# Folding products moved into the lead-in, value products waited for by halves, and reciprocal roots placed between the last scatters

## The reference, cut to what matters

```python
# x: 32 x 56 x 128; ctx: 32 x 1500 x 128; 16 heads of 8
h = layernorm(x)
q, k, v = h @ Wq + bq, ctx @ Wk + bk, ctx @ Wv + bv
att = softmax(where(causal[56, 1500] & mask, q k^T / sqrt(8), -1e9))
x = x + (att v) @ Wo + bo
# mixture of experts, 8 experts, 2 per token, capacity 280
xf = layernorm(x)
probs = softmax(xf @ gate_w + gate_b); top 2, renormalised
rank = cumsum over tokens of (token chose expert); slots past capacity dropped
h = relu(xin @ w1[e] + b1[e]); out = (h @ w2[e] + b2[e]) * weight
x = x + scatter_add(out)
```

## Time and profile before

| | |
|---|---|
| time, median of 3 runs | 176.41 us (176.31 to 176.62) |
| profiled execution, own time | 177.93 us |
| its span | 176.2 us |
| mean granted TensorE clock in it | 0.934 of 2.4 GHz |
| busy: PE (matmul) / PEld (weight loads) | 148.6 / 101.8 us |
| busy: DVE / ACT / POOL | 113.2 / 85.7 / 88.3 us |

### The profile page before, as it was taken

One profiled execution on the slowest core, in us unless ns is written; L12 is line 12 of the kernel. 1 busy time (PEld: TensorE's weight loads), 2 busy tenths in 40 slices (PEclk: granted clock), 3 DMA queues, 4 the chain that ended last, 5 costly groups with the idle time before them and its releaser, 6 DMA issues.

```text
span 176.2 us, 4560 instructions
## 1 busy us (share of the span) xinstructions
PE 148.6 (84%) x1623; PEld 101.8 (58%) x1623; DVE 113.2 (64%) x421; ACT 85.7 (49%) x188; POOL 88.3 (50%) x145
## 2 busy tenths in 40 slices
PE   6979999999999989999899796949999999894000
PEld 2436486686666767566666652414778888683000
DVE  3587747868888888787979866004385665642361
ACT  3468787589696987969766310000433333320000
POOL 5304980513586776857567466750044444656000
PEclk9999999879999999999999969996999999999555
DMA  5990299499910000001000000007300110103476
GB/s 156 335 379 4 81 407 330 127 339 335 270 53 20 31 29 9 23 13 31 15 4 26 0 22 5 22 13 199 97 15 30 37 39 15 55 24 100 180 246 228
DMA packets 10542, 19.14 MB, mean 109 GB/s; under 512 B 2044, under 2 KB 6000, under 8 KB 9880
## 3 DMA queue, kind: packets, MB, share of 16 engines
q1 hardware_dynamic: 7424, 15.12, 25.5%
q0 software_dynamic: 1632, 2.28, 4.1%
q10 hardware_dynamic: 1464, 1.45, 2.7%
HBM read 12.13 MB, written 7.91 MB: 114 GB/s over the span
## 4 chain that ended last, share of the span: by engine, by line
PE 47%; ACT 14%; issue 13%; DVE 9%; POOL 7%; DMA 6%; POOLq 1%; DVEq 0%; SPq 0%; ACTq 0%
PE bank L1250 7%; PE score_p L1049 6%; PE bank L1077 5%; ACT probsT L570 4%; ACT head_keys L514 4%; POOL slots_d L419 4%; PE score_p L1232 4%; PE bank L1232 4%; PE bank L1064 3%; PE score_p L981 3%; PE score_p L1016 3%; DMA chosen<-choice_d 2%; DMA choice_d<-rest_ow,rest_i 2%; DVE row_max L688 2%; ACT probs L561 2%
## 5 line engine op out<-in xcount | busy, mean ns | idle before, releaser
L419 POOL DMA_INDIRECT slots_d<-rec,slot_i x32 | 32.3, 1009 | 14.4 <-issue 9.3
L465 POOL DMA_INDIRECT choice_d<-ow,dst_i x16 | 15.8, 987 | 25.2 <-DVE ow L939 22.2
L981 PE MATMUL score_p<-warm 128*128 128x512 bf16 x76 | 23.1, 461 | 4.5 <-DMA slots_d<-rec,slot_i 2.4
L688 DVE TENSOR_REDUCE row_max<-score_p 128x16 f32<-128x912 f32 x16 | 17.7, 1107 | 4.8 <-PE score_p L1049 4.7
L570 ACT ACTIVATE probsT<-bank 128x512 f32<-128x512 f32 x32 | 17.6, 605 | 5.2 <-PE bank L1064 4.9
L1049 PE MATMUL score_p<-head_keys,queries 32*32 32x228 f32 (+1 forms) x384 | 19.6, 366 | 0.4 <-ACT head_keys L514 0.4
L1077 PE MATMUL bank<-vals,probsT 128*64 128x18 f32 x512 | 17.6, 212 | 2.4 <-ACT probsT L570 2.4
L1077 PEld LDWEIGHTS bank<-vals,probsT 128*64 128x64 f32 x512 | 16.1, 138 | 6.0 <-ACT probsT L570 4.5
L691 DVE TENSOR_TENSOR probs<-score_p,row_max 128x912 f32<-128x912 f32 x16 | 17.7, 1109 | 1.6
L1064 PE MATMUL bank<-ident,probs 128*128 128x128 f32 x128 | 17.7, 283 | 0.0
L981 PEld LDWEIGHTS score_p<-warm 128*128 128x128 bf16 x76 | 8.3, 114 | 15.8 <-issue 5.8
(11 more groups left out here) (153 smaller groups left out, 267.1 us busy)
## 6 DMA issues: line engine op xcount, KB each, us to landing
choice_d<-chosen SPq DMA_DIRECT2D x2, 1024.0 KB, 8.3
w_s<-w_in SPq DMA_DIRECT2D x1, 2048.0 KB, 9.6
slots_d<-keys_c SPq DMA_DIRECT2D x1, 1260.0 KB, 4.5
xg<-slots_d SPq DMA_DIRECT2D x8, 140.0 KB, 3.2
xT<-x_t_in SPq DMA_DIRECT2D x1, 1024.0 KB, 10.6
chosen<-choice_d SPq DMA_DIRECT2D x1, 1024.0 KB, 5.4
xs<-x_in SPq DMA_DIRECT2D x1, 768.0 KB, 7.4
ctxT<-ctx_t_in SPq DMA_DIRECT2D x1, 768.0 KB, 8.7
```

What stands on the lines that cost most here:

```text
L419: gp.indirect_dma_start(out=slots_d, out_offset=bass.IndirectOffsetOnAxis(ap=slot_i[:, t, k, p:p + 1], axis=0), in_=rec[:, GP * t + p, :], ...
L688: ve.reduce_max(row_max[:, p, :], heads, X).then_inc(max_d, 1)
L981: mm(to, warm[:, 0:128], warm[:], start=True, stop=True)
```

## The change

- `fold_gate` and `share_logits` move from round 1 (behind values(0)) in front of the loop, where the 5 fillers stood. `centre_gate` moves from behind scores(1) in front of it, and one filler there goes. The transposed mean gets a bank of the ring for norm(2) instead of one of the post banks, with a semaphore of its own; norm(2) now waits until it has been copied. VectorE's copies follow: gate_c in front of softmax(1), fold and shareT in front of softmax(2), statistics1(3) behind softmax(2).
- `mix(n)` waits for the first half of the probabilities in front of product 1 and for the second in front of product 17.
- In round 7, ranks(5) goes in front of output(6) and slots(5) in front of residual(6); the post banks' order follows, so that mix(14) must wait until slots(5) has read its ranks.
- GpSimd's end: power2(6) between the first and the second DMA of scatter(5), power2(7) between the second and third of scatter(6). count(6) goes to VectorE (`count_late`), behind slots(6) and before weigh_late(6).
- Fillers: other numbers, and three new places (in front of rank 6, behind output(7) with a wait for root 7, and behind the arrival of the first expert's rows).

```diff
-WARM_LEAD = (3, 2, 2, 3)
-WARM_START, WARM_PAIR = 11, 5
-WARM_TURN, WARM_MIX, WARM_Y, WARM_CHOICE, WARM_SLOTS, WARM_SCATTER, WARM_LANDING, WARM_FIRST = 2, 2, 2, 14, 3, 27, 11, 4
+WARM_START, WARM_LEAD = 11, (3, 2, 2, 2)
+WARM_TURN, WARM_TAKEN, WARM_MIX, WARM_Y, WARM_LOGITS, WARM_CHOICE, WARM_SLOTS = 2, 3, 2, 3, 12, 7, 3
+WARM_SCATTER, WARM_LANDING, WARM_ROWS, WARM_FIRST = 32, 9, 3, 4
...
# GpSimd
-                if g >= 1:
+                if 1 <= g < GROUPS - 1:
                     power2(g - 1)
             t = GROUPS - 1
             count(t - 2)
-            scatter(t - 2)
+            scatter(t - 2, 0, 1)
+            power2(t - 1)
+            scatter(t - 2, 1)
+            scatter(t - 1, 0, 2)
             power2(t)
-            count(t - 1)
-            scatter(t - 1)
+            scatter(t - 1, 2)
             scatter(t)
...
# VectorE
+            def count_late(t):
+
+                dve.wait_ge(post_d, posted("rank", t))
+                for p in range(GP):
+                    dve.wait_ge(earlier_d, GP * t + p + 1)
+                    ve.tensor_tensor(earlier[:], earlier[:], taken[:, p, :], add).then_inc(earlier_d, 1)
...
                 softmax(GP * g + 1)
+                if g == GROUPS - 1:
+                    slots(g - 2)
                 residual(g - 1)
...
             slots(t - 1)
+            count_late(t - 1)
             weigh_late(t - 1, 0)
...
# TensorE
             def mix(n):
-                pe.wait_ge(probT_ev, 2 * n + 2)
                 pe.wait_ge(ring_ev, filled("v", t))
                 to = take_post("mix", n)
                 for hp in range(HP):
+                    if hp % 4 == 0:
+                        pe.wait_ge(probT_ev, 2 * n + 1 + hp // 4)
...
             project(1)
+            centre_gate()
             keep_warm(WARM_LEAD[3], probT_b[1][:])
             scores(1)
             pe.wait_ge(mean_done, 1)
-            tr(post("mean", 0)[:, 0:B], mean[:], ident[0:B, 0:B]).then_inc(post_d, 1)
-            centre_gate()
+            pe.wait_ge(ring_ev, filled("norm", 1))
+            tr(ring("norm", 2)[:, 0:B], mean[:], ident[0:B, 0:B]).then_inc(mean_d, 1)
             transpose_probs(0)
             transpose_probs(1)
-            keep_warm(WARM_PAIR, ring("norm", 1)[:])
+            fold_gate()
+            share_logits()
...
                     values(0)
-                    fold_gate()
-                    share_logits()
...
+                if g == GROUPS - 1:
+                    ranks(g - 2)
                 output(g - 1)
                 mix(GP * g)
-                if g >= 2:
+                if 2 <= g < GROUPS - 1:
                     ranks(g - 2)
...
             mix(PAIRS - 1)
+            keep_warm(WARM_TAKEN)
             ranks(t - 1)
             keep_warm(WARM_MIX)
             turn_y(t)
             keep_warm(WARM_Y)
             output(t)
+            keep_warm(WARM_LOGITS)
+            pe.wait_ge(rs2_d, GROUPS)
             keep_warm(WARM_CHOICE)
             ranks(t)
...
             keep_warm(WARM_LANDING)
+            pe.wait_ge(xg_in[0], 16)
+            keep_warm(WARM_ROWS)
             transpose_slots(0, 0)
```

More of the change, by code:

```diff
@@ L65, in post_order @@
 def post_order():
-    uses = [("kept", 0), ("mean", 0), ("centre", 0), ("fold", 0), ("shareT", 0), ("share", 0), ("mix", 0)]
+    uses = [("kept", 0), ("centre", 0), ("fold", 0), ("shareT", 0), ("share", 0), ("mix", 0)]
     for g in range(1, GROUPS):
-        for kind, t in (("mix", 2 * g - 1), ("wo", g - 1), ("mix", 2 * g), ("rank", g - 2)):
+        behind = (("wo", g - 1), ("mix", 2 * g))
+        rank = (("rank", g - 2),)
+        for kind, t in (("mix", 2 * g - 1), *(rank + behind if g == GROUPS - 1 else behind + rank)):
             if t >= 0:
@@ L201, in build @@
         wqk_in, mask_in, wvo_in, wb_in, consts_in = (sem(n) for n in ("wqk_in", "mask_in", "wvo_in", "wb_in", "consts_in"))
-        mean_done, meanT_ev, slow_dma, slow_step = (sem(n) for n in ("mean_done", "meanT_ev", "slow_dma", "slow_step"))
+        mean_done, mean_d, meanT_ev = (sem(n) for n in ("mean_done", "mean_d", "meanT_ev"))
+        slow_dma, slow_step = sem("slow_dma"), sem("slow_step")
         slots_cleared, choices_cleared, zeros_done, empties_done = (
@@ L786, in slots, with mean_column @@
                     ve.reduce_sum(slot_i[:, t], slot_k[:], X).then_inc(slot_d, 1)
[L788 to L793, removed]
+            def count_late(t):
[3 more added lines that the diff above has]
+                    ve.tensor_tensor(earlier[:], earlier[:], taken[:, p, :], add).then_inc(earlier_d, 1)
+            def mean_column(batches):
+                dve.wait_ge(mean_d, 1)
+                ve.tensor_copy(ctxT[:, batches, S], ring("norm", 2)[:, batches]).then_inc(meanT_ev, 1)
             ve.memset(warm[:], 1.0).then_inc(warm_done, 1)
@@ L831, in _ @@
             statistics1(2)
+            dve.wait_ge(post_d, posted("centre", 0))
+            dve.wait_ge(gate_clear, 1)
+            ve.tensor_copy(gate_c[:, 0:E], post("centre", 0)[:, 0:E]).then_inc(post_read, 1)
             softmax(1)
@@ L835, in _ @@
             dve.wait_ge(ctx_in[1], 16)
-            mean_column(slice(0, 4 * GP), False)
-            statistics1(3)
+            mean_column(slice(0, 4 * GP))
             dve.wait_ge(ctx_in[2], 16)
[L839 to L842, removed]
+            mean_column(slice(4 * GP, B))
+            dve.wait_ge(post_d, posted("fold", 0))
+            ve.tensor_copy(bo_share[:], post("fold", 0)[:, E:E + 1]).then_inc(bo_share_d, 1)
+            ve.tensor_copy(wvo_s[:, WVO_FOLD:WVO_FOLD + E], post("fold", 0)[:, 0:E]).then_inc(post_read, 1)
+            dve.wait_ge(bo_share_d, 1)
+            dve.wait_ge(post_d, posted("shareT", 0))
+            ve.tensor_scalar(shareT[:], post("shareT", 0)[:], bo_share[:], None, add).then_inc(post_read, 1)
             for g in range(1, GROUPS):
@@ L845, in _ @@
                 if g == 1:
[L846 to L849, removed]
-                    dve.wait_ge(post_d, posted("shareT", 0))
-                    ve.tensor_scalar(shareT[:], post("shareT", 0)[:], bo_share[:], None, add).then_inc(post_read, 1)
+                    statistics1(3)
                     dve.wait_ge(post_d, posted("share", 0))
@@ L984, in norm @@
                 pe.wait_ge(xn_d, GP * (t + 1))
+                if t == 2:
+                    pe.wait_ge(meanT_ev, 2)
                 transposes(take_ring("norm", t), xn).then_inc(ring_d, 1)
```

## The result

The changed kernel takes 174.04 us (median of 4 executions, 173.87 to 174.77). The kernel before took 176.51 us in the same set (176.31 to 180.66). The ratio is 0.989, with a 95% interval of 0.9845 to 0.9938: 1.1% faster. Medians here take in every execution; the ratios leave out those more than 1.5% above the fastest of their kernel. Forecast were 175.1 us, range 174.0 to 176.8. The profiled execution took 174.77 us (span 173.1, mean granted clock 0.969); the forecast for such an execution, without a low stretch in the round from 33.00, was 175.1.

A forecast was written before the change was run, and what follows sets the result against it. TensorE was taken to bound the loop, busy 10.31 of 10.75 us per round. From the profiled 177.93, - 1.2 - 0.96 + 0.95 - 0.96 gave 175.76; less 0.64 for the low stretch, 175.1 us, range 174.0 to 176.8.

The forecast's parts named there:

- the two front terms: Lead-in and value products: Term A and Term B, forecast at -1.2 and -0.96 us.
- Term A: Lead-in: gate's fold and share products replace 5 fillers under VectorE's subtraction, so scores(3) starts sooner; -1.2 us, bounds 0.55 to 1.27.
- Term B: Value products: even mixes wait for only the first ScalarE copy, 0.16 us each in six mixes; -0.96 us, bounds 0 to 1.4.
- Term C: Tail after softmax(15): first scatter of group 5 sooner, but the chain through roots 6 and 7 ends later; +0.95 us, bounds +0.55 to +1.65.
- Term D: Landing of the last scatter: more fillers keep TensorE's clock at 2.4 GHz, transposes come sooner; -0.96 us, bounds 0 to 1.0.
- rival 1: Tail: its serial chain costs 1.65 us undisturbed and outweighs a small front gain, giving 177.5 us; chance 0.17.
- The low stretch from 33.00: Loop round from 33.00: profiled at 1.2 GHz, 0.64 us longer than the next; taken as absent from the timed executions.
- 2 (clock falls in spite of the fillers): Landing: the clock falls despite 32 fillers because the waits before are longer, giving 176.1 us; chance 0.15.
- 3 (GpSimd goes through): Tail: GpSimd runs on from 97.9 without waiting for VectorE, 1.1 us less, giving 174.0 us; chance 0.12.
- 4: Tail: a count_late step on VectorE is held by a running scatter, 0.5 us more, giving 175.6 us; chance 0.08.

The follow-up runs named there:

- third set: Last of three sets of runs, each on its own chip; the kernel before, against which its changed kernels were read, took 176.78 us there.

## Why the prediction was right, and where its terms were wrong

The time was 1.06 us below the forecast and only 0.04 us inside the range. The direction followed from the two front terms, as forecast; that the number stayed in the range owes something to luck, since the half waits and the low stretch were both priced too low.

**Term A, -1.2**: measured -1.0 at softmax(3) and -1.28 at the last softmax. The steps stood as written: the same TensorE time under the subtraction, and ScalarE's copies forward by 0.52 of the 0.55 us that they had stood. Of the 1.27 us the first round kept 1.0, because those copies now hold TensorE for 0.25 us; the prediction had named ScalarE's copies as what is late next, but let them reach the loop only through yT.

**Term B, -0.96: the step that was mis-sized.** It took from the row at 48.43 that a load behind a met wait comes 0.28 us after the one before. Measured are 0.13 us, and 0.31 us in each steady round instead of 0.16. Over the loop it gives 1.3 to 1.4 us, at the term's upper bound of 1.4: not six times 0.31, since what mix(2) wins is lost to the wait for the normalised rows, a wait that the term doesn't name. The 0.28 us belongs to the product in front, not to the wait: among the mixes of the loop it stands in the changed kernel only where the product in front has 224 columns, though the waits are the same in the others, and kernels with two and with eight waits in each mix have the same round. The prediction itself noted that met waits between small products cost nothing visible, and then didn't use it for the first load.

**Term C, +0.95**: +1.21 against the profile of before, +1.78 against the old order at full clock. The prediction gave +1.65 as the bound for an undisturbed old order; the second value is slightly past it. The reason for the larger one is the one named there: in the profile of before the output product in front of residual(7) ran at the low clock. Its four products at 102.48 took 1.27 us there, and 0.73 in the old tail run again. That is 0.54 of the difference; the rest is 0.3 us, by which the first woven scatter and root 6 came later than worked out (98.39 and 100.42 for scatter and choose(6), shifted back by 3.62 us, against 97.9 and 99.9), since GpSimd's weights and count of group 5 weren't done when slots(5) was. The new order is indifferent to that product, as forecast: in its second profile the product ran at the low clock too (1.11 us), and the last scatter stands 22.71 us behind the subtraction, against 22.70. Every wait forecast for this chain is in the trace, at the place forecast.

**Term D, -0.96**: -0.91 between the two profiles, the forecast number, while the forecast cause isn't shown. With the old fillers and TensorE idle for the same 2.39 us another kernel's landing took 5.13 us, so the low clock doesn't follow from that idle time alone, and where it stays away the fillers gain nothing. The prediction had this case only as a part of rival 1.

**The low stretch from 33.00, -0.64**: its absence is worth 1.4 us (1.56 at the row maximum in it, 1.43 at the next), more than twice as much. The price was read as the difference to the next round; but the undisturbed round is shorter than the next one. The same kernel's loop took 5.56 us from the row maximum of softmax(4) to that of softmax(5) without the stretch and 7.12 with it. It is in five of the fourteen profiles: three of the six with the old lead-in, two of the eight with the new one. That is too few to say that the new lead-in makes it rarer. All six timed executions with the new front and the old tail lie within 0.8 us, but two of six of the changed kernel in the third set were 1.2 to 2 us above the rest.

**Rivals.** 1 (the tail eats the lead) had the price right, 1.65 against 1.78, and the front's worth wrong: it needed A + B to stay below that, and they gave 2.7. The tail is a loss all the same. 2 (clock falls in spite of the fillers) didn't happen in the three profiles of the changed kernel. 3 (GpSimd goes through) is refuted by the waits of 1.89 and 2.54 us. 4 didn't happen: the two steps of `count_late` took 0.35 us together at 99.86, under the scatter that ran from 99.42 to 100.39. A rule of mutual exclusion as told in the Trainium skill (SBUF - State Buffer, Who interferes with whom) isn't seen in this pair. The same section of the Trainium skill also tells of a probe in which `tensor_tensor` didn't stall a DMA, and that is what these rows show.

By the profiles at full clock the change is thus about -1.3 (lead-in) and -1.4 (half waits), given back in part by +1.8 (tail), which would be -0.9; the medians say -2.5 in the first measurement and -2.6 in the third set. The missing 1.6 us have the size of one low stretch, which most executions of the kernel before seem to hold (its median in the third set is 1.7 us above its fastest, 175.05) and most of the changed kernel's don't. The half waits alone fit this: nine of their twelve timed executions lie between 175.1 and 176.3 us, near the profiled one with the stretch (175.77), and for them nothing is missing (1.4 us by the median, 1.4 by the profiles). This is argued from the spread of the times; no run shows it directly.

The best kernel found is the change without its tail: 171.99 us, 2.15 below the changed kernel and 4.8 below the one before.

## What to carry to other kernels

An idle gap next to a wait isn't the wait's until the same gap is missing where there is no wait; here it belonged to the product in front, and one wait per half cost nothing. And what a shorter wait wins reaches the end only if no later wait takes it back: of 0.35 us won in one round here nothing was left at the next transposes. Where two engines pass a chain back and forth, look first whether the short step that the other engine waits for stands behind bulk work: here a 0.7 us root stood 0.99 us behind a scatter, and the new order as a whole made the end 1.8 us later, though GpSimd began its scatters sooner. And a gain over a stretch that was profiled at a low granted clock is no gain until further executions of the same kernel show the stretch again; its price is read against the same stretch at full clock, not against its neighbour.

## What the runs showed of the hardware

Apart from the last microseconds of the span, the granted clock fell to the lower level in stretches of some microseconds in twelve of the fourteen profiled executions, at other places from one to the next; in one case the work in front was equal to the last digit. Its price was what it covered: 1.6 us in a round of the loop, 0.54 at one output product in the old tail, nothing at the same product in the new tail, where GpSimd was busy for longer.

TensorE came out of 2.35 to 2.39 us of idle time behind 27 fillers twice at a granted clock of 0.56 to 0.58 and once at 1.00, in kernels that are alike there.

On two of the chips VectorE stood for up to 4.9 us in front of single instructions, mostly the reciprocals of `divide`, and the kernel before took 7 to 8% longer than on the third. The trace names no instruction that it waited for, and what it was stays open.
